# A selective scan laid out as 32 channels by 4 states, with both directions in one unit, all drives on GpSimd, and delta and du spread by copies inside SBUF

## The reference

```
u     = silu(causal_conv(in_w_x @ seq));  z = in_w_z @ seq
delta = softplus(dt_w @ (xp_w_dt @ u) + dt_b);  B, C = xp_w_B @ u, xp_w_C @ u
h[d,n] = exp(delta[d] * A[d,n]) * h[d,n] + (delta[d] * u[d]) * B[n]      (step by step)
y[d]   = sum over n of h[d,n] * C[n]  +  u[d] * D[d];   out = out_w @ (y * silu(z))
```

## Time and profile before

| | |
|---|---|
| median of 3 runs | 40272.85 us (40259.12 to 40300.51) |
| profiled execution, its own time | 40283.3 us |
| its span in the profile | 40281.5 us |
| busy: PE, DVE, ACT, POOL | 62%, 65%, 49%, 62% of the span |
| DMA | 7230 MB, 179 GB/s |

### The profile page before, as it was taken

How to read it: one execution, slowest core, us unless ns; L and a number is a source line. 1 busy time by engine, 2 the same in 40 slices (tenths; PEclk the granted TensorE clock), 3 DMA queues, 4 the chain that set the end, 5 groups by cost and what they waited for, 6 DMA issues and landing times. The chain is left out here.

```text
span 40281.5 us, 323274 instructions
## 1 busy us (share of the span) xinstructions
PE 24925.9 (62%) x75932; PEld 7783.3 (19%) x75932; DVE 26249.4 (65%) x15920; ACT 19794.8 (49%) x25923; POOL 24988.5 (62%) x10756
## 2 busy tenths in 40 slices
PE   6666666666666666666666666666666666665384
PEld 1111111111111111111111111111111111111221
DVE  6666666666666666666666666666666666666211
ACT  5555555555555555555555555555555555554022
POOL 6666666666666666666666666666666666665000
PEclk7777777777777777777777777777777777777597
DMA  7777777777777777777777777777777777778767
GB/s 173 183 182 183 182 182 181 182 185 183 183 183 182 182 182 182 184 183 183 184 183 184 183 183 182 183 184 182 184 184 182 184 183 184 182 185 183 138 125 157
DMA packets 2491075, 7230.00 MB, mean 179 GB/s; under 512 B 444632, under 2 KB 708456, under 8 KB 2461672
## 3 DMA queue, kind: packets, MB, share of 16 engines
q1 hardware_dynamic: 2491000, 7229.05, 75.6%
HBM read 6086.95 MB, written 738.20 MB: 169 GB/s over the span
## 5 line engine op out<-in xcount | busy, mean ns | idle before, releaser
L781 POOL TENSOR_TENSOR read<-state,c_rep 128x1024 f32<-128x1024 f32 x8192 | 19168.1, 2356 | 11286.4 <-DVE state L718 11276.0
L595 ACT ACTIVATE decay<-decay,a_neg 128x1016 f32<-128x1016 f32 x5632 | 6436.3, 1143 | 15023.0 <-DMA decay<-delta_spread 15007.1
L718 DVE TENSOR_TENSOR_SCAN state<-decay,pair_ps 128x1024 f32<-128x1024 f32 x5632 | 12646.9, 2272 | 67.7
L703 DVE TENSOR_TENSOR pair_ps<-pair_ps,b_rep 128x1024 f32<-128x1024 f32 x5632 | 6723.3, 1223 | 8833.5 <-PE pair_ps L415 8829.8
L718 DVE TENSOR_TENSOR_SCAN state<-pair_ps,drive 128x1024 f32<-128x1024 f32 x2560 | 5835.3, 2279 | 1819.4 <-ACT pair_ps L598 1783.3
L765 POOL TENSOR_TENSOR drive<-drive,b_rep 128x1024 f32<-128x1024 f32 x2560 | 6016.7, 2350 | 844.7 <-DMA drive<-du_spread 844.7
L415 PE MATMUL pair_ps<-u_stack,spread 96*128 96x512 bf16 x11264 | 4035.5, 466 | 3314.9 <-DVE state L718 3287.4
L438 PE MATMUL y_bank<-read,sel_f 128*32 128x512 f32 x32768 | 4831.6, 716 | 33.2 <-POOL read L781 31.5
L381 PE MATMUL p_bank<-u,to_c 128*128 128x512 f32 x2048 | 1998.8, 1105 | 2818.7 <-ACT zs L527 2070.2
L595 ACT ACTIVATE pair_ps<-decay,a_neg 128x1016 f32<-128x1016 f32 x2560 | 2835.6, 1108 | 1361.3 <-DVE state L718 1361.2
L375 PE MATMUL p_bank<-xt,taps 128*128 128x512 f32 x4096 | 2489.2, 763 | 1042.5 <-DMA xt<-in_xs 1040.4
(11 more groups left out here) (105 smaller groups left out, 22317.9 us busy)
## 6 DMA issues: line engine op xcount, KB each, us to landing
decay<-delta_spread SPq DMA_DIRECT2D x8192, 512.0 KB, 5.2
drive<-du_spread SPq DMA_DIRECT2D x2560, 512.0 KB, 8.0
u_stack<-u_parts SPq DMA_DIRECT2D x6144, 64.0 KB, 10.2
delta_spread<-delta SPq DMA_DIRECT2D x512, 512.0 KB, 5.7
du_spread<-du SPq DMA_DIRECT2D x512, 512.0 KB, 4.2
xt<-in_xs SPq DMA_DIRECT2D x512, 256.0 KB, 14.2
rec<-o_sb SPq DMA_DIRECT2D x512, 128.0 KB, 5.8
c_img<-x SPq DMA_DIRECT2D x16, 4096.0 KB, 50.5
```

The source lines that it names most:

```text
L595: ins = nc.scalar.activation(inner(dst, d), inner(src, d), ACT.Exp, scale=a_neg[s][:, 4 * j + k:4 * j + k + 1])
L703: nc.vector.tensor_tensor(ps, ps, b_rep[d][:, :], ALU.mult).then_inc(s_drive_v, 1)
L718: nc.vector.tensor_tensor_scan(state[:, q % H_RING, ::step], a, x, 0.0, ALU.mult, ALU.add).then_inc(s_state, 1)
L781: nc.gpsimd.tensor_tensor(read[:, q % R_RING, :], state[:, q % H_RING, :], c_rep[d][:, :], ALU.mult).then_inc(s_read, 1)
```

## The change

The unit is now half a tile (4 sequences) in both directions: columns 0 to 511 forwards, 512 to 1023 backwards, so again 512 units of 16 q. The partitions hold 32 channels by 4 states: q = 4m + j has channels 32j to 32j+31 and states 4m to 4m+3. B and C come out of one small projection (`take_bc`, 64 x 512), are stored to DRAM (`store_bc`), and each quarter is read back on 128 partitions by `load_b` and `load_c`: 4 of each a unit, 512 KB each, with the source `states`, whose outermost dimension is 4 rows, each repeated 32 times. delta and du are copied within SBUF to the four blocks of 32 partitions: `spread` issues 4 copies of 32 rows for each of 4 j. So delta needs no load per q; `delta_rep` has one buffer, `du_rep` two. POOL makes all 16 drives (a ring of 4, three ahead) and reads 5 states; DVE scans each q in two instructions of 512 columns (forwards and backwards), for 11 q into PSUM, and reads those 11 from PSUM in two instructions. ACT writes every decay into PSUM, a ring of 2. The bf16 parts, their copies, the matmuls that take parts off, the spreading matmuls, and delta and du in DRAM are gone. There is one bank `p_bank`, so each projection waits until the one before is taken; `STEPS` gives the q at which PE makes and ACT takes each. `make_du` writes to SBUF at q = 5 and 7. The core of the diff (empty lines and most removed lines are left out):

```diff
+PAIRS, ROW = 16, 4
+WIDE = 2 * HALF
+USEQS = SEQS // 2
+BY_POOL = (1, 4, 7, 10, 13)
 NG = len(BY_POOL)
-D_RING, H_RING, R_RING = 4, 4, 8
-STACKS = 12
+DRIVE_RING, READ_RING, STATE_RING = 4, 8, 2
+DRIVE_AHEAD = 3
...
+STEPS = [Step("dt", REV, 1, 0, 0), Step("bc", 0, 1, 1, 1), Step("ds", FWD, 1, 4, 5),
+         Step("ds", REV, 1, 6, 7), Step("out", 0, -1, 8, 9), Step("x", FWD, 2, 11, 12),
+         Step("x", REV, 2, 12, 13), Step("z", 0, 1, 13, 14), Step("dt", FWD, 2, 14, 15)]
+SOFTPLUS = ((1, 0), (2, 1), (2, 2), (3, 3))
+DU = {FWD: 5, REV: 7}
+GATE, UD = 2, 5
+GATHER = (4, 8, 12)
...
+        delta_rep = sb("delta_rep", [P, ROW, WIDE])
+        du_rep = [sb(f"du_rep{h}", [P, ROW, WIDE]) for h in range(2)]
+        b_rep = sb("b_rep", [P, ROW, WIDE])
+        c_rep = sb("c_rep", [P, ROW, WIDE])
+        drive = sb("drive", [P, DRIVE_RING, WIDE])
+        state = sb("state", [P, STATE_RING, WIDE])
+        read = sb("read", [P, READ_RING, WIDE])
+        decay = [pb(f"decay{n}", [P, WIDE]) for n in range(2)]
+        state_ps = pb("state_ps", [P, WIDE])
+        y_bank = pb("y_bank", [P, HALF])
+        p_bank = pb("p_bank", [P, HALF])
...
-            def group_rows(dram, q):
-                k, j = group_of(q)
-                return bass.AP(dram.tensor, dram.offset + (32 * j + 8 * k) * PX,
-                               [[0, NS], [PX, 8], [1, PX]])
-            def load_pair(d, q):
-                sp.dma_start(decay[:, q % D_RING, :], group_rows(spill["delta"][d], q)
-                             ).then_inc(s_pair[q % D_RING], 16)
...
+            def store_bc(h, d):
+                sp.dma_start(spill["bc"][h][:, px(d)], bc[32 * d:32 * d + 32, :]).then_inc(s_bc, 16)
+            def spread(dst, src, j, sem):
+                for n in range(4):
+                    sp.dma_start(dst[32 * n:32 * n + 32, j, :], src[32 * j:32 * j + 32, :]).then_inc(sem, 16)
+            def states(dram, m):
+                return bass.AP(dram.tensor, dram.offset + 4 * m * WIDE,
+                               [[WIDE, 4], [0, 32], [1, WIDE]])
+            def load_delta(h, j):
+                spread(delta_rep, e_one, j, s_delta[j])
+            def load_du(h):
+                for j in range(ROW):
+                    spread(du_rep[h], e_log, j, s_du[h][j])
+            def load_b(h, m):
+                sp.dma_start(b_rep[:, m, :], states(spill["bc"][h][0:NS, :], m)).then_inc(s_b[m], 16)
+            def load_c(h, m):
+                sp.dma_start(c_rep[:, m, :], states(spill["bc"][h][NS:2 * NS, :], m)).then_inc(s_c[m], 16)
...
+                    at_least(sp, s_ysum, ROW * U)
+                    load_c(h, 3)
+                    if w_next2 is not None:
+                        sp.wait_ge(s_proj, FIRST_USES + USES * U - 1)
+                        load_x(i + 1, h)
                     if w_next is not None:
+                        sp.wait_ge(s_evac, taken["bc", 0])
+                        store_bc(1 - h, FWD)
+                        sp.wait_ge(s_drive, PAIRS * U + 4)
+                        store_bc(1 - h, REV)
+                        sp.wait_ge(s_bc, 32 * (U + 2))
+                        load_b(1 - h, 0)
+                        sp.wait_ge(s_ysum, ROW * U + 1)
+                        load_c(1 - h, 0)
+                        sp.wait_ge(s_drive, PAIRS * U + 8)
+                        load_b(1 - h, 1)
+                        sp.wait_ge(s_evac, taken["ds", REV])
+                        load_du(1 - h)
+                        sp.wait_ge(s_ysum, ROW * U + 2)
+                        load_c(1 - h, 1)
+                    if h == 1:
+                        store(i, 0, taken["out", 0])
+                    elif prev is not None:
+                        store(i - 1, 1, taken["out", 0])
                     if w_next is not None:
+                        sp.wait_ge(s_drive, PAIRS * U + 12)
+                        load_b(1 - h, 2)
+                        for j in range(2):
+                            sp.wait_ge(s_decay, PAIRS * U + 13 + j)
+                            load_delta(1 - h, j)
+                        sp.wait_ge(s_ysum, ROW * U + 3)
+                        load_c(1 - h, 2)
+                        for j in range(2, 4):
+                            sp.wait_ge(s_decay, PAIRS * U + 13 + j)
+                            load_delta(1 - h, j)
+                        sp.wait_ge(s_drive, PAIRS * U + 16)
+                        load_b(1 - h, 3)
...
-            def spread_du(U, d, q, pairs):
-                k, j = group_of(q)
-                if q == 0:
-                    pe.wait_ge(s_stack, 16 * STACKS * (U + 1))
-                at_least(pe, s_state, pairs + q - 1)
-                for h in range(2):
-                    mm = nc.tensor.matmul(pair_ps[q % 2][:, px(h)], spread[0:96, k, :],
-                                          u_stack[d][:, j, px(h)], start=True, stop=True)
-                mm.then_inc(s_du_b, 1)
...
+            def make_decay(U, s, q):
+                m, j = group_of(q)
+                if m == 0:
+                    act.wait_ge(s_delta[j], 64 * (U + 1))
+                at_least(act, s_state, 2 * PAIRS * U + 2 * q - 2)
+                nc.scalar.activation(inner(decay[q % 2][:, :]), inner(delta_rep[:, j, :]), ACT.Exp,
+                                     scale=a_neg[s][:, ROW * j + m:ROW * j + m + 1]).then_inc(s_decay, 1)
...
+            def make_du(h, d, copied):
+                dve.wait_ge(s_evac, copied)
+                nc.vector.tensor_tensor(e_log[:, px(d)], p_bank[:, :], u[h][:, px(d)],
+                                        ALU.mult).then_inc(s_evac, 1)
+            def scan(U, h, q):
+                dve.wait_ge(s_decay, PAIRS * U + q + 1)
+                dve.wait_ge(s_drive, PAIRS * U + q + 1)
+                n = pool_before(q)
                 if q in BY_POOL:
+                    at_least(dve, s_read_g, NG * U + n - STATE_RING + 1)
+                    out = state[:, (NG * h + n) % STATE_RING, :]
                 else:
+                    out = state_ps[:, :]
+                for d in range(2):
+                    if q not in BY_POOL:
+                        at_least(dve, s_read_v, 2 * NV * U + 2 * vector_before(q) - 1 + d)
+                    step = 1 if d == FWD else -1
+                    nc.vector.tensor_tensor_scan(out[:, px(d)][:, ::step],
+                                                 decay[q % 2][:, px(d)][:, ::step],
+                                                 drive[:, q % DRIVE_RING, px(d)][:, ::step], 0.0,
+                                                 ALU.mult, ALU.add).then_inc(s_state, 1)
+            def read_state(U, q):
+                m, j = group_of(q)
+                dve.wait_ge(s_c[m], 16 * (U + 1))
+                at_least(dve, s_ysum, ROW * U + m - 1)
+                for d in range(2):
+                    dve.wait_ge(s_state, 2 * PAIRS * U + 2 * q + d + 1)
+                    nc.vector.tensor_tensor(read[:, q % READ_RING, px(d)], state_ps[:, px(d)],
+                                            c_rep[:, m, px(d)], ALU.mult).then_inc(s_read_v, 1)
...
+            def make_drive(U, h, tile, q):
+                m, j = group_of(q)
+                if m == 0:
+                    pool.wait_ge(s_du[h][j], 64 * (tile + 1))
+                if j == 0:
+                    pool.wait_ge(s_b[m], 16 * (U + 1))
+                at_least(pool, s_state, 2 * PAIRS * U + 2 * (q - DRIVE_RING) + 2)
+                nc.gpsimd.tensor_tensor(drive[:, q % DRIVE_RING, :], du_rep[h][:, j, :],
+                                        b_rep[:, m, :], ALU.mult).then_inc(s_drive, 1)
+            def read_state(U, h, q):
+                m, j = group_of(q)
+                pool.wait_ge(s_state, 2 * PAIRS * U + 2 * q + 2)
+                pool.wait_ge(s_c[m], 16 * (U + 1))
+                at_least(pool, s_ysum, ROW * U + m - 1)
+                nc.gpsimd.tensor_tensor(read[:, q % READ_RING, :],
+                                        state[:, (NG * h + pool_before(q)) % STATE_RING, :],
+                                        c_rep[:, m, :], ALU.mult).then_inc(s_read_g, 1)
```

More of the change, by code:

```diff
@@ L575, in softplus @@
                     act.wait_ge(s_soft, 4 * U + 1)
+                    if not first:
+                        for j in range(ROW):
+                            act.wait_ge(s_du[1 - h][j], 64 * (tile + h))
                     nc.scalar.activation(e_one[:, :], e_abs[:, :], ACT.Identity,
@@ L635, in body @@
+            def body(i, prev, cur, nxt):
+                for U, h, w_prev, w_next, w_next2 in units(i, prev, cur, nxt):
+                    rows = numbered(i, h, nxt)
+                    taken = {(s.kind, s.d): after for s, _, _, after in rows}
                     for q in range(PAIRS):
                         ahead = q + AHEAD
-                        if ahead >= PAIRS and w_next is not None:
-                            decay_pair(U + 1, 1 - d, w_next, ahead - PAIRS, pairs + PAIRS)
-                        elif ahead < PAIRS and ahead not in BY_POOL:
```

(41 more changed lines are left out.)

709 lines of the change are left out of this document (263 added, 446 removed).

## The result

The changed kernel takes 39370.67 us (median of 4 runs, 39347.61 to 39385.49), the kernel before 40265.99 us on the same chip (4 runs, 40191.47 to 40300.51): the ratio is 0.978, with a 95% interval of 0.9763 to 0.9797. It is faster by 2.2%. The forecast was 52600 us, so even the sign was wrong.

What follows compares the result with a forecast made beforehand. The prediction took the queue of four DMA engines carrying B and C to bound the changed kernel: 512 units of 96.3 us (49306), 3164 after and 122 before give 52592, so 52600 us; range 37000 to 57500.

Steps and rivals of the forecast that it cites:

- How many engines: DMA copies are cut along their outermost dimension, so load_b and load_c run on 4 engines each, 32 rows an engine.
- always-same-four choice: All load_b and load_c copies were taken to run on the same 4 DMA engines, the lowest-numbered ones.
- What a row costs on such an engine: A 4096-byte row of B or C takes 278 ns on its DMA engine: 71.2 us a unit.
- forecast's own sign of being wrong: B and C copies leaving 16 marks and landing in 3 us, or a lone 512 KB one landing in 5 us.
- the waits of POOL for du: POOL's waits for du_rep would be among the longest, with those for b_rep and ACT's for delta_rep.
- The rows of the spreads: du and delta copies within SBUF: 32 copies x 2 rows x 0.308 us on each of the four engines, 19.7 us a unit.
- The sum: Four engines' unit of 96.3 us: B and C 71.2, du and delta 19.7, the rest 2.4, empty about 3.
- 4 engines, but quick ones: Rival: four DMA engines at the stores' pace, 164 ns a row, 67 us a unit, 37600 us; chance 0.13, at about 39700.
- the sum of 55.4 us: DVE's work a unit: scans 38.7 us, 22 reads 14.7, two make_du and a gate 2.0.
- The stalls at du: DVE waits for ACT's copy of delta out of p_bank: 0.35 us after scan 5, 1.7 after scan 7.
- POOL, ACT, SP: Work a unit: POOL 49.4 us, ACT about 32, both hidden under DVE's 57.5; SP issues 45 copies in 28 us.
- The rival on 16 engines: Rival: B and C copies run on all 16 engines, DVE sets the unit, 34000 us, within 32700 to 36000; chance 0.15.

Runs made afterwards that it cites:

- run 7: Changed kernel with the B and C copies' source 8 rows outermost, so 8 DMA engines: 35734.87 us, ratio 0.89; its table sets busiest engines' summed work against measured units.
- run 1: Changed kernel with a stage in front that only copies, groups of differing outermost dimension, each alone: 4 outermost 102 GB/s, 8 126, 32 418; no kernel time given.
- run 8: Changed kernel with groups of 18 KB-row copies in front, to neighbouring or spread partitions: from DRAM 195 or 347, 207 or 417, 133 or 246 GB/s; no kernel time given.
- run 10: run 4's kernel with the du products after pairs 6 and 8 in place of 5 and 7: 31010.5 us, ratio 0.7723, 54.2 us a unit.
- run 4: Changed kernel with partitions ordered channel by state: B and C copies 32 outermost on 16 engines, spreads writing every fourth partition: 32937.66 us, ratio 0.818.
- run 5: Changed kernel with only the B and C copies put on 16 engines, spreads still to blocks of 32 partitions: 33181.48 us, ratio 0.823, 58.4 us a unit.
- run 3: Changed kernel with only SP's order changed, delta issued ahead of B and C copies: 39542.73 us, ratio 0.9819, 70.9 us a unit.
- run 6: Changed kernel with only the spreads writing every fourth partition, B and C still on four engines: 36385.32 us, ratio 0.9023, 64.7 us a unit.
- run 11: run 4's kernel with du products after pairs 6 and 9, each spread then one copy repeating rows four times, not four copies: 33424.97 us, ratio 0.8327.

## Why the prediction was wrong, step by step

- *How many engines.* Right. The 11 marks gave "cut along the outermost dimension", and the changed kernel shows the 624 marks a unit that were forecast and shares of 0.25. The always-same-four choice is borne out by the sums of run 7's table. The Trainium skill's rule (DMA: Bandwidth & Descriptors, section "Why a DMA increments its semaphore by 16 and not by 1") takes the largest number up to 16 that divides both slowest dimensions. The trace agrees for 4, 2, 8 and 10 engines (shares 0.25, 0.13, 0.51 and 0.63 in run 1).
- *What a row costs on such an engine: the step that failed.* I took 278 ns and wrote "the limit is an engine's own, and 4 engines alone would not speed up". It measured 161 (102 GB/s on four engines, run 1). The forecast's own sign of being wrong, a lone copy of 512 KB in 5 us, is what run 1 shows: 5.1 us for each of such copies. With it went what hung on a long queue: the waits of POOL for du were to be among the longest and come to 95 us in the whole run, and the DMA share is 0.49 at 124 GB/s, not near 0.4 at 92. The error was in what the rows could carry. 298 ns at 10 engines did show that idle neighbours do not help that copy, but the copy went to 40 neighbouring partitions, and those set its pace (run 8). The spreading loads, 16 outermost with 8 rows each, were a slow shape as well (run 1: 235 against 418 GB/s to the same 128 partitions). 256 rows x 117 ns less is 30 us a unit. What picks the quick pace for four engines that write all 128 partitions, no run shows; that it is the shape of the copy and not an engine's own limit, runs 1 and 8 do.
- *The rows of the spreads.* 308 ns forecast, 352 measured in the window of du: 2.8 us too few. *The sum.* With the two measured prices it is 69.1 us, and the unit took 70.5. The mechanism was right (four engines' queue sets the unit, delta waits behind B and C); one term of it was off by 30 us and carried the sign with it.
- *The rival "4 engines, but quick ones"* gave the time: 67 us at 164 ns, 71 at 180, measured 70.5. Its reason did not hold as written: the limit is not one that all engines share, since 16 engines run at 418 or at 235 GB/s by the shape alone (run 1). That it comes so near 70.5 is in part luck: B and C went at 161 ns and not at 180, and the spreads at 352 ns made up for more than half of that. And the stated range, 37000 to 57500, holds 39371 only because it was stretched down for this rival; the forecast's own 50000 to 57500 does not. I had put its break-even at 184 ns and gave it 0.13. The evidence for it was on the table: the store of delta at 25 GB/s an engine. I set it aside for being a store. The Trainium skill's figure for an engine (DMA: Bandwidth & Descriptors, section "Specifications") is about 27 GiB/s, which makes an estimate of 141 ns a row. That was nearer than my price; the quickest loads of run 1 took 160.
- *DVE.* Scans at 1.21 us and reads at 0.67 are as forecast, but the sum of 55.4 us is too large: run 10 has units of 54.2 us in which DVE is busy 94%, so 51 us. Of the changed kernel, DVE's timeline where it does not wait (start, us for all):

```profile
10014.49 2.33 DVE L659 TENSOR_TENSOR_SCAN state_ps<-decay,drive 128x512 f32<-128x512 f32 x2
10016.73 1.27 DVE L671 TENSOR_TENSOR read<-state_ps,c_rep 128x512 f32<-128x512 f32 x2
10017.92 2.34 DVE L659 TENSOR_TENSOR_SCAN state_ps<-decay,drive 128x512 f32<-128x512 f32 x2
```

From start to start two scans and two reads take 3.43 us, where their mean times add up to 2 x 1.213 + 2 x 0.673 = 3.77: each starts some 0.09 us before the one ahead has ended. For the 57 instructions of a unit that is 4.9 us, and 55.4 becomes 50.5. I compared a sum of means with a busy time of the page (51.3), which counts overlap once. *The stalls at du* of 0.35 and 1.7 us: the second is 1.69 in the unit that the timeline shows; the first is 4.65, because the copy on ACT also waits for TensorE's result, which I had not counted.
- *POOL, ACT, SP.* POOL is 48.9 us busy of a unit (25031.3 / 512) where I had 49.4, hidden as said. SP issued 16 copies in 10.09 us, as forecast, where the queue was not full.
- *The rival on 16 engines* would have been right had the copies been cut otherwise: 34000 forecast, 32938 measured in run 4.

So the gain of 2.2% is a small difference of two large things. Without narrow copies and with strided spreads the new layout is worth 14 us a unit against the kernel before (72.3 to 57.9, run 4), and 18 with du's products moved as well (54.2, run 10). I put that down to the 8 MB of delta loads a unit that no longer wait for scans; no run takes them out alone. The narrow copies of B and C give 12 of it back (70.5 against 58.4, run 5).

## What to carry to other kernels

Cut a copy so that all 16 engines share it, and try more than one such cut: the same bytes to the same 128 partitions ran at 418 GB/s with 32 outermost and at 235 with 16 (run 1). Look at which partitions it writes: from DRAM, 32 or 64 neighbouring ones run at about half the rate of spread ones, and of copies within SBUF that run alone only those with both sides spread gained (run 8). A rate read from one copy is the price of that shape, and before it is carried over to another with fewer engines, look for the row of the trace that speaks against it, a faster copy above all. Where a queue's total sets the time, changing the order of its entries moves the wait and keeps its length (run 3).

## What the runs showed that I had not expected

- Repeated rows to the same 128 partitions run at 418 GB/s with 32 outermost and at 235 with 16 outermost (run 1). Which engines then meet was not tried.
- Four engines keep 26 GB/s each, eight fall to 16 (126 / 8). By the cut the four write one block of 32 partitions each and the eight one of 16. The port rule alone, as cited, does not tell these two apart; that stays open.
- SBUF to SBUF, 32 neighbouring partitions give 190 GB/s when alone (run 8), and 177 within the changed kernel. Writing every fourth partition gives 213 in the kernel (run 6) and 186 alone (run 8), a difference that stays open.
- Fewer and larger copies were slower than four times as many small ones (run 11).
